# Fourth-stage statistics taken a stage earlier, and half a butterfly stage moved from GpSimd to VectorE

## What is computed

```
xq  = act_quant(fwht(layernorm(x)))          # Walsh-Hadamard over 512, then 8 bits per row
h   = silu(xq @ wq_gate.T) * (xq @ wq_up.T)  # ternary weights, width 2048
out = act_quant(fwht(h)) @ wq_down.T         # Walsh-Hadamard over 2048, then 8 bits per row
x   = x + out
act_quant: scale = 127 / clip(max|row|, 1e-5); round(row * scale) / scale
```

## Time and profile before

| | |
|---|---|
| median of three runs | 722.65 us |
| the profiled execution: span, first to last instruction | 719.6 us |
| median above the span (launch and end) | 3.05 us |
| busy in the span: TensorE, VectorE, ScalarE, GpSimd | 654.6, 587.3, 468.7, 392.7 us |
| stage d, bodies 0 to 15 and drain | about 449 to 719.6 us |

### The profile page before, as it was taken

How to read it: one execution, slowest core, us unless ns; L and a number is a source line. 1 busy time by engine, 2 the same in 40 slices (tenths; PEclk the granted TensorE clock), 3 DMA queues, 4 the chain that set the end, 5 groups by cost and what they waited for, 6 DMA issues and landing times.

```text
span 719.6 us, 12514 instructions
## 1 busy us (share of the span) xinstructions
PE 654.6 (91%) x4067; PEld 374.6 (52%) x4098; DVE 587.3 (82%) x1358; ACT 468.7 (65%) x949; POOL 392.7 (55%) x291
## 2 busy tenths in 40 slices
PE   1688899999999999997999999887999999999996
PEld 0365566666666676842434444443544545544543
DVE  6889899999998887376676774788999989999875
ACT  3737567766776655367778732566787788778744
POOL 2023122324132313257998951079999999899970
PEclk9999999999999999999999999999999999999999
DMA  9971333324231323629999931434556655665621
GB/s 221 260 239 23 82 97 81 108 84 111 67 111 23 111 66 81 235 53 274 247 298 209 235 66 23 87 70 88 108 103 118 131 102 104 136 126 106 114 60 45
DMA packets 173132, 88.22 MB, mean 123 GB/s; under 512 B 150547, under 2 KB 152595, under 8 KB 172053
## 3 DMA queue, kind: packets, MB, share of 16 engines
q1 hardware_dynamic: 167188, 71.94, 43.7%
q10 hardware_dynamic: 3408, 11.27, 4.8%
q0 software_dynamic: 2480, 4.33, 3.3%
HBM read 51.20 MB, written 4.19 MB: 77 GB/s over the span
## 4 chain that ended last, share of the span: by engine, by line
PE 44%; DVE 26%; ACT 9%; issue 8%; POOL 6%; DMA 5%; SPq 1%; POOLq 0%; DVEq 0%; ACTq 0%
PE ps L1807 10%; PE ps L1661 7%; PE ps L1733 7%; PE ps L1751 6%; DMA arena<-arena 4%; PE ps L1676 4%; DVE X L1095 3%; DVE arena L1185 2%; PE ps L1787 2%; POOL arena L535 2%; POOL arena L536 2%; DVE y_sm L1490 2%; PE ps L1879 2%; ACT arena L862 2%; PE ps L1847 2%
## 5 line engine op out<-in xcount | busy, mean ns | idle before, releaser
L1661 PE MATMUL ps<-arena 128*128 128x256 f16 x1408 | 159.9, 273 | 10.4 <-DVE arena L1185 6.7
L463 POOL TENSOR_TENSOR arena<-arena 128x256 f16<-128x256 f32 x88 | 57.7, 676 | 180.4 <-ACT arena L634 180.0
L1661 PEld LDWEIGHTS ps<-arena 128*128 128x128 f16 x1408 | 135.7, 98 | 35.5 <-DVE arena L1185 10.4
L535 POOL TENSOR_TENSOR arena<-arena 128x1024 f32<-128x1024 f32 x44 | 103.7, 2358 | 43.7 <-DVE arena L1464 39.3
L1807 PE MATMUL ps<-arena 128*128 128x512 bf16 x486 | 116.9, 383 | 10.5 <-ACT arena L833 7.7
L536 POOL TENSOR_TENSOR arena<-arena 128x1024 f32<-128x1024 f32 x44 | 104.0, 2363 | 0.0
L1807 PEld LDWEIGHTS ps<-arena 128*128 128x128 bf16 x512 | 48.1, 98 | 69.0 <-DVE arena L1456 9.9
L1676 PE MATMUL ps<-arena 128*128 128x512 f16 x352 | 80.1, 384 | 3.5 <-POOL arena L463 3.5
L627 ACT ACTIVATE arena<-ps,gs 128x256 f32<-128x256 f32 x88 | 40.7, 466 | 52.5 <-PE ps L1661 52.5
L1879 PE MATMUL ps<-arena 128*128 128x512 bf16 x251 | 59.1, 379 | 2.0 <-ACT arena L906 1.8
L1733 PE MATMUL ps<-arena 128*128 128x512 f16 x256 | 59.7, 387 | 0.0
(11 more groups left out here) (158 smaller groups left out, 1211.2 us busy)
## 6 DMA issues: line engine op xcount, KB each, us to landing
arena<-in_ctx_t SPq DMA_DIRECT2D x7, 1024.0 KB, 6.3
arena<-in_wg_t SPq DMA_DIRECT2D x16, 256.0 KB, 3.8
arena<-in_wu_t SPq DMA_DIRECT2D x16, 256.0 KB, 4.4
arena<-in_wd_t SPq DMA_DIRECT2D x16, 256.0 KB, 4.9
arena<-in_ctx_n SPq DMA_DIRECT2D x4, 1024.0 KB, 9.8
arena<-in_wu_t ACTq DMA_DIRECT2D x4, 1024.0 KB, 6.4
arena<-in_wd_t ACTq DMA_DIRECT2D x4, 1024.0 KB, 6.0
out_x<-X SPq DMA_DIRECT2D x16, 256.0 KB, 2.6
```

The lines of the kernel that those rows point to most:

```text
L463: nc.gpsimd.tensor_tensor(hl[:, c, at:at + 2 * P], b_h[n % 4], hh[:, c, at:at + 2 * P], ALU.subtract).then_inc(b_hl_r, 1)
L535: nc.gpsimd.tensor_tensor(b[:, :, 0, :], a[:, :, 0, :], a[:, :, 1, :], ALU.add).then_inc(d_bfp, 1)
L1661: last = M(bank(n % 2)[:, 2 * P * i:2 * P * i + 2 * P], W[:, b, c * P:c * P + P], part[:, b, at:at + 2 * P], start=(b == 0 and part is xhT ...
```

## The change

1. Statistics (bn_stats, bn_aggr) of stage d's tiles 0 to 13 are taken in stage c, d_stats(k-3) at the end of each body, those of tiles 14 and 15 in body 0 of stage d. They are kept for all 16 tiles; variance plus epsilon, root and shift are done in two parts of eight tiles instead of once per tile.
2. pool_stage(j, 2) keeps only its addition; last_subtraction(j) on VectorE does the other half. VectorE's body now begins with first_stage(k-2, 2) and (k-2, 3), then last_subtraction(k-3), back_max(k-3, 0), d_hidden(k, 0), d_low(k+1), back_max(k-3, 1), back_scales(k-3); the rest stays in order without stats and d_center. Before GpSimd writes HD it waits for last_subtraction of the tile before.
3. front_scales has four operations instead of six, back_scales four instead of five; ScalarE's d_round waits for the third of the four.

The core of the diff:

```diff
@@ GpSimd
-                elif k < NT - 2:
-                    root("d", k - NT + 4, k % 2)
+                elif k == NT - 4:
+                    d_roots(0)
@@ pool_stage
+                if s == 1:
+                    wait(pool, d_bfs, j)
...
-                nc.gpsimd.tensor_tensor(b[:, :, 1, :], a[:, :, 0, :], a[:, :, 1, :], ALU.subtract).then_inc(d_bfp, 1)
+                if s < 2:
+                    nc.gpsimd.tensor_tensor(b[:, :, 1, :], a[:, :, 0, :], a[:, :, 1, :], ALU.subtract).then_inc(d_bfp, 1)
@@ GpSimd d_body
-                if on(k + 2):
-                    root("d", k + 2, u)
+                if at(k, 0):
+                    d_roots(1)
@@ VectorE c_body
                 if on(k - 2):
                     add_readout(k - 2, u)
+                if on(k - 3):
+                    d_stats(k - 3)
+                if at(k, NT - 5):
+                    d_variances(0)
@@ VectorE, new
+            def last_subtraction(j):
+
+                dve.wait_ge(d_bfp, 5 * j + 4)
+                wait(dve, d_yr, 2 * j)
+                V.tensor_tensor(Y[:, 2 * D:4 * D], HD[:, 0:2 * D], HD[:, 2 * D:4 * D], ALU.subtract).then_inc(d_bfs, 1)
@@ VectorE d_body
-                if rounding:
-                    back_max(k - 3, w, 0)
                 if on(k - 2):
                     first_stage(k - 2, 2)
                     first_stage(k - 2, 3)
                 if rounding:
-                    back_max(k - 3, w, 1)
+                    last_subtraction(k - 3)
+                    back_max(k - 3, w, 0)
                 if mid:
                     d_hidden(k, u, 0)
                 if front and not at(k, 0):
                     d_low(k + 1)
                 if rounding:
+                    back_max(k - 3, w, 1)
                     back_scales(k - 3, w)
                 if mid:
                     d_hidden(k, u, 1)
                 if whole:
                     d_lo(k, 0)
-                if ahead:
-                    stats("d", k + 2, u)
+                if at(k, 0):
+                    dve.wait_ge(c_add, NT)
+                    d_stats(NT - 2)
+                    d_stats(NT - 1)
+                    d_variances(1)
                 if whole:
                     d_lo(k, 1)
...
-                if ahead:
-                    d_center(k + 2, u)
+                if at(k, 1):
+                    d_shifts(1)
@@ VectorE d_drain
                 for n in range(4):
                     h_rest(n)
+                last_subtraction(13)
                 back_max(13, 1, 0)
@@ back_scales
-                V.tensor_reduce(c[3], y_sm[:, u, 0:2], AX.X, ALU.max).then_inc(d_ysm, 1)
+                V.tensor_scalar(c[4], c[0], Q_EPS / ISQ_I1, c[1], ALU.max, ALU.max).then_inc(d_ysm, 1)
                 dve.wait_ge(d_ysm, n + 3)
-                V.tensor_scalar(c[4], c[3], ISQ_I1, Q_EPS, ALU.mult, ALU.max).then_inc(d_ysm, 1)
+                V.tensor_scalar(c[5], c[4], 1.0 / 127.0, None, ALU.mult).then_inc(d_ysm, 1)
                 dve.wait_ge(d_ysm, n + 4)
-                V.reciprocal(c[5], c[4]).then_inc(d_ysm, 1)
-                V.tensor_scalar(c[7], c[4], 1.0 / 127.0, wscale[:, 2:3], ALU.mult, ALU.mult).then_inc(d_ysm, 1)
-                dve.wait_ge(d_ysm, n + 5)
-                V.tensor_scalar(c[6], c[5], 127.0 * ISQ_I1, None, ALU.mult).then_inc(d_ysm, 1)
+                V.reciprocal(c[6], c[5]).then_inc(d_ysm, 1)
+                V.tensor_scalar(c[7], c[5], wback[:, 2:3], None, ALU.mult).then_inc(d_ysm, 1)
```

More of the change, by code:

```diff
@@ L66, in fused_blocks @@
         thr = sb("thr", [P, 3])
-        nthr = sb("nthr", [P, 3])
+        wback = sb("wback", [P, 3])
         cmx = sb("cmx", [P, B, 16])
@@ L181, in fused_blocks @@
         st_step, st_rstd = {}, {}
-        for g in "abcd":
+        for g in "abc":
             st_step[g], st_rstd[g] = sem(g + "_stat"), sem(g + "_rstd")
@@ L445, in root, with d_roots @@
                 nc.gpsimd.tensor_tensor(rstd[r][:, u, :], ve[r][:, u, :], mhalf[:, :], ALU.pow).then_inc(st_rstd[g], 1)
+            def d_roots(part):
+                first, end = D_PARTS[part]
+                pool.wait_ge(d_var, part + 1)
+                nc.gpsimd.tensor_tensor(rstd_d[:, first:end, 0], ve_d[:, first:end, 0], mhalf[:, :].to_broadcast([P, end - first]),
+                                        ALU.pow).then_inc(d_root, 1)
             pool.wait_ge(const_in, 32)
@@ L850, in d_silu @@
                 i = 4 * k + n
+                if n == 0:
+                    act.wait_ge(d_fsm, 4 * k + 4)
                 act.wait_ge(d_gu, i + 1)
@@ L1380, in c_body, with d_stats, d_variances, d_shifts @@
                 if at(k, NT - 1):
+                    d_shifts(0)
                     front_scales(0, 0)
-                    stats("d", 3, 1)
                 if at(k, NT):
-                    d_norm(2, 0)
+                    d_norm(2)
                     add_readout(NT - 1, 1)
                     d_low(1)
-                    d_norm(3, 1)
+                    d_norm(3)
+            def d_stats(j):
+                u = j % 2
+                wait(dve, d_stat, 2 * j - 2)
+                V.bn_stats(bn["b"][:, u, :], tile_of(X, j)).then_inc(d_stat, 1)
+                dve.wait_ge(d_stat, 2 * j + 1)
+                V.memset(carrier["b"][:, u:u + 1], 0.0)
+                V.bn_aggr(mv_d[:, j, :], bn["b"][:, u, :]).then_inc(d_stat, 1)
+            def d_variances(part):
+                first, end = D_PARTS[part]
+                dve.wait_ge(d_stat, 2 * end)
+                V.tensor_scalar(ve_d[:, first:end, 0], mv_d[:, first:end, 1], LN_EPS, None, ALU.add).then_inc(d_var, 1)
+            def d_shifts(part):
+                first, end = D_PARTS[part]
+                dve.wait_ge(d_root, part + 1)
+                V.scalar_tensor_tensor(shift_d[:, first:end, 0], mv_d[:, first:end, 0], -1.0, rstd_d[:, first:end, 0],
+                                       ALU.mult, ALU.mult).then_inc(d_shift, 1)
+            def d_normalised(j):
+                dve.wait_ge(d_root, 1)
+                V.tensor_scalar(d_xn[j % 2], tile_of(X, j), mv_d[:, j, 0:1], rstd_d[:, j, :],
+                                ALU.subtract, ALU.mult).then_inc(d_xn_r, 1)
             def front_scales(j, u):
-                n = 6 * j
-                c = [f_sm[:, u, i:i + 1] for i in range(6)]
+                n = 4 * j
+                c = [f_sm[:, u, i:i + 1] for i in range(4)]
                 dve.wait_ge(d_f, j + 1)
@@ L1517, in d_body @@
                 w = 1 - u
-                front, mid, whole, back, rounding, out_part, ahead = on(k + 1), on(k), on(k) and not at(k, NT - 1), on(k - 1), on(k - 3), on(k - 4), on(k + 2) and not (at(k, 0) or at(k, 1))
-                if rounding:
-                    back_max(k - 3, w, 0)
+                front, mid, whole, back, rounding, out_part = on(k + 1), on(k), on(k) and not at(k, NT - 1), on(k - 1), on(k - 3), on(k - 4)
                 if on(k - 2):
```

70 lines of the change are left out of this document (36 added, 34 removed).

## The result

The kernel after takes 757.11 us (median of four runs, 755.67 to 757.84), the kernel before on the same chip 722.53 us (722.03 to 723.34): a ratio of 1.048, with a 95% interval from 1.046 to 1.050. That is slower, as forecast, but by 34.6 us where 12.3 were forecast, and outside the range.

The account below looks back on a forecast made before the run. A loop through VectorE and ScalarE, without GpSimd, was taken to set the 15.61 us tile. Steady tiles +14.2, head -0.6 and drain -1.3 gave +12.3, so 735.0 us, range 727 to 746.

Parts of the forecast that it names:

- for the two that go I take 0.18: VectorE's front_scales in a steady tile: five small operations take 0.60 us, and dropping two saves 0.18.
- The loop: Steady fourth-stage tile, through VectorE and ScalarE: period 16.85 us against 15.61, so +14.2 over twelve tiles.
- The 0.59 of the new opening order: Head of VectorE's body: first_stage now waits for ScalarE's odd_evac behind y_whole, +0.59 us per tile.
- Collision of last_subtraction: Steady tiles: VectorE's subtraction comes before GpSimd's next operation, so price in the loop 0, bounds 0 and 2.36 us.
- Third stage: Statistics moved there fit in VectorE's 2.04 us idle per tile: cost nothing, or 14 us without that cover.
- Head: Start of the fourth stage: added statistics 1.1 us, against the root's wait of 1.25 and statistics gone: -0.6.
- Drain: From 674.32 to the end: one GpSimd subtraction fewer, one collision, shorter scale chains: -1.3 us, bounds -2.4 and 0.
- this is the path: Drain: GpSimd runs without a break from 674.32 until late_stage at 698.12, so one subtraction fewer gives -2.36 us.
- rival 4: TensorE's clock falls in the new loop: up to +21 us more, 756; once in three tiles, 742; chance 0.12.
- Rival 1: Steady tiles: GpSimd was the real limit and its relief makes the kernel faster, 715 us; chance 0.08.
- Rivals 2 and 3: VectorE's additions and removals cancel, 722 or 721, chance 0.03; only one new wait appears, +5, 728, chance 0.12.
- The step from span to median: Whole kernel: the median lies 3.05 us above the profiled span, as launch and end, and this stays.

## Why the prediction was wrong in size and right in direction

The parts of a tile, forecast and measured: subtraction with its new order and less statistics and scales +1.24 forecast, +1.38 measured; the merged operation 0 forecast, +1.35 measured.

- **The failed step** is the sentence "for the two that go I take 0.18". It priced front_scales by the number of its small operations and took the merged one for one more of 0.1 to 0.2. What the runs show in its place: the merged operation stands until GpSimd's current one ends, 1.67 us in a steady tile. The 22.0 us that the span missed (34.3 less 12.3) are 12 x (18.31 - 16.99) = 15.8 for it, 12 x 0.14 = 1.7 for the rest of the tile, 0.7 that I had taken off for the last tile, 0.6 in the head and 3.2 in the drain. I had checked the new subtraction for exactly this collision, with the earlier trace rows, and did not ask it of the smallest instruction in the change. The same term was also a little short without the collision: with the pair split, the reduction of front_scales starts at 603.93 and first_stage at 605.15, so the small operations take 1.22 - 0.68 = 0.54 by the forecast's own way of counting (0.60 before). The forecast's 0.60 less 0.18 had 0.42. That is 0.12 of the 0.14 by which the rest of the tile missed.
- **The loop**, without that operation, was right: 16.85 forecast, 16.99 measured. Its first_stage waits 0.53, d_lo(k,1) 0.52 (0.6 forecast for each), d_hidden(k,3) 0.92 (1.0), GpSimd over 2 us per tile. The 0.59 of the new opening order was taken away in two ways and gave 0.62 each time. That 0.5 of the statistics' 1.01 would turn into idle time is shown by the kernel with statistics and scales alone.
- **Collision of last_subtraction**: no price in steady tiles, as said. VectorE comes first, and GpSimd's first addition takes 3.19 instead of 2.36, at a place where it had waited 2.65 already.
- **Third stage**: nothing, as said: from one tile's maximum of the scores to the next it is 7.33 us before (411.17 to 418.50) and after (404.04 to 411.37). This maximum still waits for TensorE; it waits less, because the statistics now stand in that gap:

```profile
404.04 0.69 DVE L1370 TENSOR_REDUCE c_sm<-ps 128x1 f32<-128x512 f32 x1 [1.22 <-PE ps L1781]
```

- **Head**: -0.6 forecast, 0 measured. Body 2 holds the longest L1445, 2.2 us above the 0.21 that it takes while GpSimd idles; the parts of this term were not separated further:

```profile
478.28 2.39 DVE L1445 TENSOR_SCALAR f_sm<-wback,f_sm 128x2 f32<-128x2 f32 x1
```

  The mark also hides something here. Stage 0 starts when first_stage is done; before, a maximum that costs 1.13 stood ahead of first_stage in the body, and now it stands behind. Counted from the opening of the body, the head is therefore about 1.1 longer and the drain only 0.7 (1.9 less 1.13).

- **Drain**: -1.3 forecast, +1.9 measured. The step that failed here is "this is the path": the forecast took GpSimd for the path, since it ran without a break up to late_stage. It was one of two chains that ended together in the kernel before, GpSimd at 695.72 + 2.36 = 698.08 and last_stages on VectorE at 698.00. The second chain runs from ScalarE's first y_round in body 15 over odd_evac and first_stage to VectorE's low parts of the last tile, from there through TensorE's products, and ends with last_odd_evac and last_stages. Before:

```profile
676.70 1.15 ACT L862 ACTIVATE arena<-arena,y_sm 128x1024 f32<-128x1024 f32 x1 [2.16 <-DVE y_sm L1504]
684.77 2.47 DVE L1513 TENSOR_TENSOR arena<-ps,arena 128x512 f16<-128x512 f32 x4
696.08 0.60 ACT L893 ACTIVATE arena<-ps 128x512 f32<-128x512 f32 x1 [3.31 <-PE ps L1856]
697.32 0.68 DVE L1472 TENSOR_TENSOR arena<-ps,arena 128x512 f32<-128x512 f32 x1
```

  And after:

```profile
711.50 1.15 ACT L879 ACTIVATE arena<-arena,y_sm 128x1024 f32<-128x1024 f32 x1 [4.02 <-DVE y_sm L1548]
719.31 2.48 DVE L1557 TENSOR_TENSOR arena<-ps,arena 128x512 f16<-128x512 f32 x4
730.62 0.60 ACT L913 ACTIVATE arena<-ps 128x512 f32<-128x512 f32 x1 [2.28 <-PE ps L1904]
731.86 0.68 DVE L1508 TENSOR_TENSOR arena<-ps,arena 128x512 f32<-128x512 f32 x1
732.46 1.22 DVE L1518 TENSOR_TENSOR arena<-arena 128x1024 f32<-128x1024 f32 x1
```

  From the low parts (h_rest, L1513 and L1557) to last_odd_evac it is 11.31 us in both, and from late_stage to the end 21.5. What grew is the way from stage 0 of tile 13 to the low parts: 684.77 - 674.32 = 10.45 before, 719.31 - 706.75 = 12.56 after, +2.11. In it ScalarE's y_round waits for back_scales. Between first_stage and these stand now the subtraction and both maxima, where before only one maximum stood. The runs place it: this way takes 12.57 with the subtraction alone, 12.55 with the pair split, 11.42 with the first maximum put back in front, and 10.44 with statistics and scales alone. So it is the subtraction (0.98) and the moved maximum (1.13), not the merged operation; the 1.13 is only the shift of the mark told under the head. GpSimd is done at 727.72 + 2.35 = 730.07, 2.4 us before late_stage (732.46), so its relief gives no more than the 0.20 by which late_stage follows the low parts sooner (13.15 in place of 13.35). It was relieved little, too: two of its operations of 2.36, at 706.75 and 721.99, take 3.27 and 3.34 beside VectorE's subtractions. Relieving one engine where two chains tie gives nothing as long as the other stays, and lengthening the other costs.
- **Rivals**: the clock (rival 4) did not come: 1.00 was granted in the steady tile, and the dip of 0.89 in 496 to 512 is the same as in the earlier trace rows. Rival 1, GpSimd as the limit, falls as well: with the subtraction alone GpSimd has 2.36 less to do in a tile, and the period grows by 1.88; with the pair merged in the kernel of statistics and scales GpSimd's work is unchanged, and the period grows by 0.59. Rivals 2 and 3 fall with the two waits, which both came.
- **The step from span to median** (3.05) held as a number (757.11 less 753.9 is 3.2) but was misnamed. The profiled execution of the kernel after took 755.67 with a span of 753.9, so launch and end are 1.8; the rest is that the profiled execution was quicker than the median.

The kernel with statistics and scales alone is the better version of the two halves: 0.994 of before, where the whole change is 1.048. What would take it below 15.1 us a tile is open.

## What to carry to other kernels

Merging small operations is not free because they are small: before two one-column operations on SBUF become one of several columns, look whether GpSimd works at that time, since the merged one may stand until GpSimd's operation is over, and put it, if it must be, where GpSimd waits. Price every instruction that a change rewrites against the other engines, not only the large one that it moves. And where an engine seems to be the path of a drain because it never pauses, look for the second chain that ends at the same time.

## What the hardware showed that I had not expected

- A VectorE tensor_scalar of two or of three columns, SBUF to SBUF, is excluded by a GpSimd operation (0.48, 0.92, 1.67 and up to 2.39 us, each time to within 0.03 us of GpSimd's end in the rows compared); the same with one column takes 0.20 us beside a GpSimd subtraction of 2.37.
- The same exclusion is at work in the third stage, once, on eight columns:

```profile
410.07 0.76 DVE L1420 TENSOR_SCALAR ve_d<-mv_d 128x8 f32<-128x8 f32 x1
```
```profile
409.65 1.15 POOL L504 TENSOR_TENSOR arena<-arena 128x512 f16<-128x512 f32 x1
```

  They end at 410.83 and 410.80. The second operation of this line, at 454.48 with GpSimd idle, takes 0.17:

```profile
454.48 0.17 DVE L1420 TENSOR_SCALAR ve_d<-mv_d 128x8 f32<-128x8 f32 x1
```

  The exclusion fell into VectorE's wait for the scores and cost nothing.
- GpSimd's root of eight columns at once takes 1.67 us, of one column 0.55 in the median: three times the price for eight times the work.
